# Two looked-up couples instead of three, warmed TensorE and fewer DMA additions in a field-pair recommendation tower

## The chip, the cores and the metric

The kernel is one launch on one core of a Trainium2 chip. The metric is the device time in microseconds. The core has five engines, each with its own in-order queue of instructions: TensorE (PE, matmuls; PEld is its weight load), VectorE (DVE), ScalarE (ACT), GpSimd (POOL) and SyncE (SP, which here only starts DMAs). They meet through semaphores. SBUF and PSUM are the two on-chip memories; TensorE writes only to PSUM, and GpSimd here reads and writes only SBUF.

## The reference

512 samples have 40 fields; each field has a table of 64-wide rows and one id per sample. For each of the 780 pairs of fields the row of the one goes through a 64 x 64 matrix of its own and is multiplied with the row of the other. The 780 values and 16 dense inputs go through three dense layers.

```python
e = jnp.stack([tbl_0[ids[:, 0]], tbl_1[ids[:, 1]], ...], axis=1)   # 512 x 40 x 64
vi, vj = e[:, i_idx, :], e[:, j_idx, :]                            # the 780 pairs
z = einsum('bpe,bpe->bp', einsum('bpd,pde->bpe', vi, W), vj)
h = concatenate([z, dense_ctx], axis=1)
h = maximum(h @ W_top1 + b_top1, 0.0)
h = maximum(h @ W_top2 + b_top2, 0.0)
y = h @ W_top3
```

## The kernel before

**Couples of fields.** The 40 fields are handled as 20 couples, each 128 numbers (two fields of 64) for 512 samples. They are taken from the last couple (fields 38 and 39) to the first. "Couple u" is the u-th to arrive, `k = KP - 1 - u` its place in the model. `E` is a ring of six slots that holds a couple as 128 x 512, fields down the partitions and samples across.

**Two ways to fetch a couple.** Couples 0 to 2 (`LOOKED_UP = 3`) come from small tables (1000 or 1250 rows), which are loaded whole. VectorE compares the ids with row numbers and so writes "codes", 125 x 512 matrices of zeros and ones (`encode`, L485); TensorE multiplies each part of the table with its code (`look_up_fields`, L550). There are 20, 18 and 16 such look-ups. The ids of the first couple are spread over the partitions by two matmuls (L641) and copied to SBUF by ScalarE (L421); those of the others are loaded by DMA, once per couple, ahead of its tables (L315, L319). The other couples are gathered: GpSimd starts eight indirect DMAs for each (two fields, four batches of 128 samples; `gather`, L369), and TensorE turns the rows with four transposes (`transpose_fields`, L561). ScalarE copies each couple out of PSUM into `E` (L400) and DMAs place pieces of it in `E4`.

**The main loop.** `order()` yields 37 couples of "groups" (74 groups, numbered n; a group is a set of field pairs), 13 "batched" units and the points at which couples of fields arrive. For a group TensorE makes two steps of products (`products`, L599) in a PSUM ring of three, VectorE multiplies each with other fields (`multiply`, L507), and seven groups later TensorE sums the result with ones (`reduce_two`, L624). For some couples of groups the two halves of the product are added before, so that the sum takes 8 instructions and not 16: by GpSimd (`ADDED_COUPLES`, L380) or by an accumulating DMA that GpSimd starts (`DMA_COUPLES`, L377). In a batched unit TensorE makes four steps (L582), VectorE multiplies (L521), and ScalarE sums eight fields of each with 16 short instructions per half (L416). The batched units multiply with the wide rows, samples down the partitions, of couples 0 to 3; looked-up couples are turned for this by TensorE (`turn_rows`, L570) and copied (L407).

**What sets the order.** Every engine follows `order()`. GpSimd runs through the groups in turn and puts ahead of group n all gathers with `gather_due(u, i) <= n`, which is `GATHER_LEAD` groups before they are wanted. Its DMA and its own additions stand in the same queue. `ahead(u)` says how many groups before its first use a couple of fields is turned. `SPLIT_FIRST` is the order in which ScalarE copies couples 0 to 3; the first group needs couples 2 and 3, the second also 1 and 0.

## Time and profile before

| | before |
|---|---|
| median of 3 runs | 329.62 us (329.34 to 329.81) |
| profiled execution: time, span | 329.33 us, 327.5 us |
| TensorE busy | 315.8 us, 96% |
| VectorE busy | 258.3 us, 79% |
| GpSimd busy | 234.9 us, 72% |
| ScalarE busy | 219.4 us, 67% |

A busy share is a mean over stages. TensorE's matmuls overlap and their ends are modelled, so 96% isn't a full engine. GpSimd's figure leaves out the 0.3 us between two gathers. What bounds a stage is read from what ended the idle time of an engine there, in brackets at the end of a timeline's row.

### The profile page before, as it was taken

The page shows a single profiled execution, that of the slowest core. Times are in us where ns is not written, and L with a number is a line of the kernel's source. Part 1 is how long each engine was busy: PE and PEld are TensorE (multiplying, and loading weights), DVE is VectorE, ACT ScalarE, POOL GpSimd, SP SyncE. Part 2 cuts the span into 40 slices and gives each one's busy share as a digit, 9 for nine tenths or more (in the row PEclk, how much of TensorE's full clock was granted, in tenths as well). Part 3 has the DMA queues.
Part 4 walks back from the last instruction along what each step waited for, and adds up shares of the span by engine and source line. Part 5 has one row for each costly group of instructions (what it writes and reads, how often), then busy time and mean ns, then how long its engine had stood idle before and what let it go on. Part 6 is the DMA issues. An engine that isn't in the chain of part 4 may idle for free.

```text
span 327.5 us, 5637 instructions
## 1 busy us (share of the span) xinstructions
PE 315.8 (96%) x1488; PEld 111.6 (34%) x1488; DVE 258.3 (79%) x270; ACT 219.4 (67%) x1699; POOL 234.9 (72%) x196
## 2 busy tenths in 40 slices
PE   6999999999999999999999999999999999999996
PEld 1232343333323324333224333332233333234442
DVE  3798379778888898998999899989999987960000
ACT  3000220049984999699999999999999999810022
POOL 6787777777788767779879998999999773940000
PEclk9999999999999999999999999999999999999999
DMA  3555825242579799994333223223212200000000
GB/s 96 142 151 147 236 73 148 68 133 70 127 163 186 185 209 256 285 258 115 79 83 88 84 56 108 79 77 79 73 42 82 64 1 0 3 2 0 0 0 0
DMA packets 19320, 33.16 MB, mean 101 GB/s; under 512 B 4948, under 2 KB 5080, under 8 KB 19288
## 3 DMA queue, kind: packets, MB, share of 16 engines
q1 hardware_dynamic: 12344, 21.52, 22.1%
q0 software_dynamic: 5792, 9.71, 15.5%
q10 hardware_dynamic: 1152, 1.57, 1.7%
q8 instruction: 12, 0.20, 0.3%
q14 instruction: 20, 0.16, 0.2%
HBM read 22.82 MB, written 0.00 MB: 70 GB/s over the span
## 4 chain that ended last, share of the span: by engine, by line
PE 73%; ACT 10%; DMA 8%; DVE 5%; issue 3%; SPq 1%; DVEq 0%
PE ps_t L599 33%; PE ps_z L624 12%; PE ps_t L582 12%; ACT batched L416 9%; DMA prod<-in_tbl 8%; PE ps_t L633 6%; DVE prod L507 4%; PE ps_e L561 3%; PE ps_t L550 2%; PE ps_t L688 2%; PE ps_e L633 2%; DVE batched L521 1%; ACT E L400 1%; PE ps_e L570 1%; PE ps_t L666 0%
## 5 line engine op out<-in xcount | busy, mean ns | idle before, releaser
L416 ACT ACTIVATE batched<-batched 128x64 f32<-128x64 f32 x832 | 198.8, 253 | 0.0
L507 DVE TENSOR_TENSOR prod<-ps_t,E 128x1024 f32<-128x1024 f32 x148 | 171.0, 1217 | 16.6 <-PE ps_t L599 16.0
L416 ACT ACTIVATION_READ_ACCUMULATOR batched<-batched 128x1 f32 x832 | 165.9, 199 | 0.0
L369 POOL DMA_INDIRECT rows<-in_tbl,ids_sb x128 | 125.5, 981 | 35.1 <-issue 34.7
L599 PE MATMUL ps_t<-E,w_sb 64*128 64x512 f32 x592 | 145.3, 614 | 4.2 <-ACT E L400 2.0
L380 POOL TENSOR_TENSOR prod<-prod 128x1024 f32<-128x1024 f32 x38 | 89.9, 2373 | 13.2 <-DVE prod L507 12.7
L599 PEld LDWEIGHTS ps_t<-E,w_sb 64*128 64x128 f32 x592 | 51.1, 185 | 86.9 <-issue 57.0
L521 DVE TENSOR_TENSOR batched<-ps_t,wide_rows 128x1024 f32<-128x1024 f32 x52 | 60.1, 1218 | 7.9 <-PE ps_t L582 7.6
L582 PE MATMUL ps_t<-w_sb,E 64*128 64x512 f32 x208 | 48.4, 603 | 0.0
L624 PE MATMUL ps_z<-prod,quads 128*32 128x512 f32 x320 | 48.1, 602 | 0.0
L400 ACT ACTIVATE E<-ps_e 128x512 f32<-128x512 f32 x18 | 10.6, 591 | 49.2 <-PE ps_e L561 36.0
L485 DVE TENSOR_SCALAR prod<-prod,first_row_f 125x512 f32<-125x512 int32 (+1 forms) x54 | 24.0, 504 | 8.4 <-ACT prod L421 4.0
L582 PEld LDWEIGHTS ps_t<-w_sb,E 64*128 64x128 f32 x208 | 18.5, 186 | 30.1 <-issue 21.0
L633 PE MATMUL ps_t<-z,w_sb 128*128 128x512 f32 (+1 forms) x42 | 18.4, 592 | 0.0
L624 PEld LDWEIGHTS ps_z<-prod,quads 128*32 128x32 f32 x320 | 8.7, 108 | 28.1 <-issue 15.0
L550 PE MATMUL ps_t<-prod 125*64 125x512 f32 x68 | 16.9, 596 | 0.4 <-DMA prod<-in_tbl 0.4
L624 PE MATMUL ps_z<-prod,halves 128*32 128x512 f32 x80 | 17.2, 598 | 0.0
L550 PE MATMUL ps_e<-prod 125*64 125x512 f32 x40 | 13.2, 751 | 0.6 <-DMA prod<-in_tbl 0.6
L377 POOL DMA_DIRECT2D prod<-prod x10 | 10.2, 1023 | 2.4 <-DVE prod L507 2.4
L633 PEld LDWEIGHTS ps_t<-z,w_sb 128*128 128x128 f32 (+1 forms) x42 | 8.0, 190 | 10.1 <-issue 10.1
L561 PE MATMUL ps_e<-ident,rows 128*128 128x128 f32 x64 | 10.5, 286 | 0.8 <-ACT wide_rows L407 0.8
L561 PEld LDWEIGHTS ps_e<-ident,rows 128*128 128x128 f32 x64 | 6.7, 140 | 12.8 <-issue 12.8
(43 smaller groups left out, 69.2 us busy)
## 6 DMA issues: line engine op xcount, KB each, us to landing
w_sb<-in_w_units SPq DMA_DIRECT2D x50, 256.0 KB, 2.7
prod<-prod POOLq DMA_DIRECT2D x10, 512.0 KB, 5.8
E<-E SPq DMA_DIRECT2D x48, 64.0 KB, 2.4
rows<-in_tbl,ids_sb POOLq DMA_INDIRECT x128, 3.3
w_sb<-in_w SPq DMA_DIRECT2D x7, 256.0 KB
E<-E ACTq DMA_DIRECT2D x24, 64.0 KB, 3.7
prod<-in_ids_by_field SPq DMA_DIRECT2D x2, 512.0 KB, 4.4
prod<-in_tbl SPq DMA_DIRECT2D x3, 312.5 KB
```

Of the source, the lines that this page charges most:

```text
L369: pool.indirect_dma_start(rows_of(u, b)[:, f * DIM:(f + 1) * DIM], None, tables[2 * k + f], bass.IndirectOffsetOnAxis(ap=ids_sb[:, col:col ...
L380: pool.tensor_tensor(prod[:, n % P_RING, 0, :, :], prod[:, n % P_RING, 0, :, :], prod[:, n % P_RING, 1, :, :], ALU.add).then_inc(halves_ad ...
L416: last = act.activation(products, products, ACT.Copy, accum_out=zt[:, b, at:at + 1])
L485: dve.tensor_scalar(codes[0:used, j % CODE_RING, :], wide, float(c), first_row_f[0:used, i:i + 1], ALU.subtract, ALU.is_equal).then_inc(co ...
L507: dve.tensor_tensor(prod[:, n % P_RING, s, :, :], ps_t[:, step % STEPS, :, :], multiplier, ALU.mult).then_inc(product_ready, 1)
L521: dve.tensor_tensor(batched[:, at % B_RING, :, :, :].rearrange("p i f n -> p i (f n)"), ps_t[:, step % STEPS, :, :], wide_rows[:, b, None, ...
L550: pe.matmul(e_bank[u][half:half + DIM, :], small[f][:, c, :], codes[0:splits[f][0], j % CODE_RING, :], start=(c == 0), stop=(c == splits[f ...
L561: last = pe.transpose(e_bank[u][:, b * P:(b + 1) * P], rows_of(u, b), ident[:])
L582: last = pe.matmul(ps_t[:, step % STEPS, i, :], E[at:at + DIM, slot_of(k), b * P:(b + 1) * P], w_sb[at:at + DIM, m % W_RING, :], start=Tru ...
L599: last = pe.matmul(ps_t[:, step % STEPS, j, :], w_sb[at:at + DIM, m % W_RING, col:col + P], E[at:at + DIM, slot_of(pairs_of(n)[s][j]), :], ...
L624: last = pe.matmul(ps_z[to:to + 32, :], ones, prod[:, g % P_RING, s, j, :], start=(q == 0 and s == 0), stop=((q == PER_CHUNK // 2 - 1 or n ...
L633: last = pe.matmul(h1_bank[m], w1_sb[0:used, c, m * P:(m + 1) * P], z[0:used, c, :], start=(c == 0), stop=(c == ALL_CHUNKS - 1))
```

## The change

- Two couples are looked up instead of three (38 look-ups instead of 54). Couple 2 is gathered as couple 3 is, with eight more gathers (144 instead of 136). Couple 2 is turned before the first look-up of couple 1 and couple 3 before its seventeenth.
- Three matmuls of the identity with itself stand ahead of TensorE's first work.
- The codes of couple 0 are made straight from PSUM; ScalarE's two copies are gone.
- ScalarE's queue starts the load of one of the first two tables. SyncE starts the weights when three of the four tables and the ids have landed.
- Couples 7 and 8 of groups (groups 14 to 17) are not halved any more; `DMA_COUPLES` is 10, 11, 13.
- Couple 6 of the fields is turned one group earlier; couples are copied in the order 0, 2, 3, 1; wide rows are turned twice instead of three times, one group later; gathers are due 8 groups ahead instead of 7.

```diff
-FETCHED_AT = 8
-LOOKED_UP = 3
+FETCHED_AT = (0, 16)
+LOOKED_UP = 2
+WARM_UP = 3
-GATHER_LEAD = 7
+GATHER_LEAD = 8
-DMA_COUPLES = (7, 8, 10, 11, 13)
+DMA_COUPLES = (10, 11, 13)
 def ahead(u):
-    return 0 if u in (6, 7) else 1 if u < 12 else 2
+    return 0 if u == 7 else 1 if u < 12 else 2
-SPLIT_FIRST = (0, 1, 3, 2)
+SPLIT_FIRST = (0, 2, 3, 1)
-WIDE_AFTER = (0, 1, 2)
+WIDE_AFTER = (1, 2)
...
 # SyncE
-            for u in range(LOOKED_UP):
-                if u > 0:
-                    for f in looked_up[2 * u - 2:2 * u]:
-                        sp.wait_ge(small_loaded[f], 16)
-                    sp.dma_start(ids_wide[:, 2 * u:2 * u + 2, :].bitcast(I32),
...
+            load_small(looked_up[0])
+            for f in looked_up[0:2]:
+                sp.wait_ge(small_loaded[f], 16)
+            for u in range(1, LOOKED_UP):
+                sp.dma_start(ids_wide[:, 2 * u:2 * u + 2, :], ids_by_field[None, looked_up[2 * u]:looked_up[2 * u] + 2, :].
+                             to_broadcast([P, 2, BATCH])).then_inc(wide_loaded[u], 16)
                 for f in looked_up[2 * u:2 * u + 2]:
+                    load_small(f)
+                sp.wait_ge(wide_loaded[u], 16)
...
-            for f in looked_up:
+            for f in looked_up[:-1]:
                 sp.wait_ge(small_loaded[f], 16)
...
 # ScalarE
+            f = looked_up[1]
+            act.dma_start(small[f], tables[f].rearrange("(p c) n -> p c n", p=splits[f][0])).then_inc(small_loaded[f], 16)
...
-            for i in range(2):
-                act.wait_ge(ids_spread, i + 1)
-                act.activation(ids_wide[:, i, :], ps_t[:, 0, i, :], ACT.Copy).then_inc(ids_spread_copied, 1)
...
 # VectorE
-                        dve.wait_ge(ids_spread_copied, i + 1)
-                    wide = ids_wide[0:used, i, :] if u == 0 else ids_wide[0:used, i, :].bitcast(I32)
+                        dve.wait_ge(ids_spread, i + 1)
+                    wide = ps_t[0:used, 0, i, :] if u == 0 else ids_wide[0:used, i, :]
...
 # TensorE
-                    if u == LOOKED_UP - 1 and j - before == FETCHED_AT:
-                        transpose_fields(LOOKED_UP)
+                    if u == 1 and j - before in FETCHED_AT:
+                        transpose_fields(LOOKED_UP + FETCHED_AT.index(j - before))
...
+            for _ in range(WARM_UP):
+                pe.matmul(ps_z[:, 0:P], ident[:], ident[:], start=True, stop=True)
```

**TensorE, from its first look-up to its first products.** Before (L550 is a look-up, L561 a transpose of gathered rows, L599 a product; `small_loaded34` is the table of field 34):

```order
L550 MATMUL ps_e<-prod 64x512 [waits code_ready,small_loaded38,sums_ready]
L550 MATMUL ps_e<-prod 64x512 [waits code_ready,small_loaded39]
L550 MATMUL ps_e<-prod 64x512 [waits code_ready] x18
L550 MATMUL ps_t<-prod 64x512 [waits code_ready,small_loaded36]
L550 MATMUL ps_t<-prod 64x512 [waits code_ready,small_loaded37]
L550 MATMUL ps_t<-prod 64x512 [waits code_ready] x16
L550 MATMUL ps_t<-prod 64x512 [waits code_ready,small_loaded34]
L550 MATMUL ps_t<-prod 64x512 [waits code_ready,small_loaded35]
L550 MATMUL ps_t<-prod 64x512 [waits code_ready] x6
L561 MATMUL ps_e<-ident,wide_rows 128x128 [waits e_copied,wide_rows_loaded3]
L561 MATMUL ps_e<-ident,wide_rows 128x128 x3
L550 MATMUL ps_t<-prod 64x512 [waits code_ready] x8
```

The same place now (L553, L564 and L602 are the three lines above):

```order
L553 MATMUL ps_e<-prod 64x512 [waits code_ready,small_loaded38,sums_ready]
L553 MATMUL ps_e<-prod 64x512 [waits code_ready,small_loaded39]
L553 MATMUL ps_e<-prod 64x512 [waits code_ready] x18
L564 MATMUL ps_t<-ident,wide_rows 128x128 [waits wide_rows_loaded2]
L564 MATMUL ps_t<-ident,wide_rows 128x128 x3
L553 MATMUL ps_t<-prod 64x512 [waits code_ready,small_loaded36]
L553 MATMUL ps_t<-prod 64x512 [waits code_ready,small_loaded37]
L553 MATMUL ps_t<-prod 64x512 [waits code_ready] x14
L564 MATMUL ps_e<-ident,wide_rows 128x128 [waits e_copied,wide_rows_loaded3]
L564 MATMUL ps_e<-ident,wide_rows 128x128 x3
L553 MATMUL ps_t<-prod 64x512 [waits code_ready] x2
L602 MATMUL ps_t<-E,w_sb 128x512 [waits e_copied,w_loaded0]
```

The look-ups of fields 34 and 35 are gone, and four transposes of couple 2's gathered rows stand before those of field 36.

**GpSimd, from its first gather on.** Before (each L369 row is a run of gathers, L377 an accumulating DMA; `transposed` is TensorE's count of couples turned):

```order
L369 DMA wide_rows<-in_tbl,ids_sb 128x64 [waits ids_loaded]
L369 DMA wide_rows<-in_tbl,ids_sb 128x64 x7
L369 DMA rows<-in_tbl,ids_sb 128x64 x32
L369 DMA rows<-in_tbl,ids_sb 128x64 [waits transposed]
L369 DMA rows<-in_tbl,ids_sb 128x64 x7
L369 DMA rows<-in_tbl,ids_sb 128x64 [waits transposed]
L369 DMA rows<-in_tbl,ids_sb 128x64 x7
L369 DMA rows<-in_tbl,ids_sb 128x64 [waits transposed]
L369 DMA rows<-in_tbl,ids_sb 128x64 x7
L369 DMA rows<-in_tbl,ids_sb 128x64 [waits transposed]
L369 DMA rows<-in_tbl,ids_sb 128x64 x4
L377 DMA prod<-prod 128x1024 [waits product_ready]
```

Now (L372 gathers, L380 is the DMA), the first and then the last rows ahead of the first DMA:

```order
L372 DMA wide_rows<-in_tbl,ids_sb 128x64 [waits ids_loaded]
L372 DMA wide_rows<-in_tbl,ids_sb 128x64 x15
L372 DMA rows<-in_tbl,ids_sb 128x64 x32
L372 DMA rows<-in_tbl,ids_sb 128x64 [waits transposed]
```

```order
L372 DMA rows<-in_tbl,ids_sb 128x64 [waits transposed]
L372 DMA rows<-in_tbl,ids_sb 128x64 x7
L372 DMA rows<-in_tbl,ids_sb 128x64 [waits transposed]
L372 DMA rows<-in_tbl,ids_sb 128x64 x3
L380 DMA prod<-prod 128x1024 [waits product_ready]
```

The eight gathers of couple 2 stand ahead of all others, and 92 gathers stand ahead of the first DMA (for group 20), where 69 stood ahead of the first one before (for group 14).

**TensorE at couple 6 of the fields.** Before (L624 is a sum of products; `rows_loaded2` are couple 6's rows):

```order
L624 MATMUL ps_z<-prod,halves 32x512 [waits product_ready]
L624 MATMUL ps_z<-prod,halves 32x512 x7
L599 MATMUL ps_t<-E,w_sb 128x512 [waits product_ready,e_copied,w_loaded4]
L599 MATMUL ps_t<-E,w_sb 128x512
L599 MATMUL ps_t<-E,w_sb 128x512 [waits product_ready]
L599 MATMUL ps_t<-E,w_sb 128x512
L561 MATMUL ps_e<-ident,rows 128x128 [waits e_copied,rows_loaded2]
L561 MATMUL ps_e<-ident,rows 128x128 x3
```

Now:

```order
L627 MATMUL ps_z<-prod,halves 32x512 [waits product_ready]
L627 MATMUL ps_z<-prod,halves 32x512 x7
L564 MATMUL ps_e<-ident,rows 128x128 [waits e_copied,rows_loaded2]
L564 MATMUL ps_e<-ident,rows 128x128 x3
L602 MATMUL ps_t<-E,w_sb 128x512 [waits product_ready,e_copied,w_loaded4]
L602 MATMUL ps_t<-E,w_sb 128x512
L602 MATMUL ps_t<-E,w_sb 128x512 [waits product_ready]
L602 MATMUL ps_t<-E,w_sb 128x512
```

The transposes moved ahead of group 8.

## Rows read from the trace of the kernel before

**Rows 1.** Timeline of TensorE: start, us, instructions [idle before <-releaser].

```profile
33.40 3.65 PE L550 MATMUL ps_t<-prod 125*64 125x512 f32 x16
37.87 1.99 PE L599 MATMUL ps_t<-E,w_sb 64*128 64x512 f32 x8 [0.81 <-ACT E L400]
...
50.42 0.66 PE L561 MATMUL ps_e<-ident,rows 128*128 128x128 f32 x4
```

**Rows 2.** Chain that ended last, in order of time: start, us, what.

```profile
19.37 9.82 DMA prod<-in_tbl
```

**Rows 3.** Granted clock in 40 slices; weight loads of the look-ups.

```profile
PEclk9999999999999999999999999999999999999999
...
13.36 0.24 PEld L550 LDWEIGHTS ps_e<-prod 125*64 125x64 f32 x2 [0.62 <-DVE prod L485]
14.09 0.14 PEld L550 LDWEIGHTS ps_e<-prod 125*64 125x64 f32 x2 [0.49 <-issue]
```

**Rows 4.** Timeline of GpSimd.

```profile
3.33 1.10 POOL L369 DMA_INDIRECT wide_rows<-in_tbl,ids_sb  x1 [1.28 <-DMA ids_sb<-in_ids_t]
...
19.10 1.18 POOL L369 DMA_INDIRECT rows<-in_tbl,ids_sb  x1 [0.30 <-issue]
...
35.42 0.94 POOL L369 DMA_INDIRECT rows<-in_tbl,ids_sb  x1 [0.30 <-issue]
...
92.56 1.02 POOL L377 DMA_DIRECT2D prod<-prod  x1
```

**Rows 5.** Timeline of TensorE at the transposes of couples 6 to 9.

```profile
58.94 1.99 PE L599 MATMUL ps_t<-E,w_sb 64*128 64x512 f32 x8
60.86 0.66 PE L561 MATMUL ps_e<-ident,rows 128*128 128x128 f32 x4
...
69.61 0.66 PE L561 MATMUL ps_e<-ident,rows 128*128 128x128 f32 x4
...
78.40 0.66 PE L561 MATMUL ps_e<-ident,rows 128*128 128x128 f32 x4
...
88.54 0.66 PE L561 MATMUL ps_e<-ident,rows 128*128 128x128 f32 x4
```

**Rows 6.** Row gathers issued in 24:35, 60:92 and 65.3:66.3: count, median us to landing.

```profile
rows<-in_tbl,ids_sb POOLq DMA_INDIRECT x8, 6.0
...
rows<-in_tbl,ids_sb POOLq DMA_INDIRECT x27, 2.6
...
rows<-in_tbl,ids_sb POOLq DMA_INDIRECT x1, 2.7
```

**Rows 7.** The chain at couple 13: start, us, what.

```profile
137.91 0.60 ACT E L400
138.50 21.02 ACT batched L416 x176
```

**Rows 8.** Groups by form: xcount | busy, mean ns | idle before.

```profile
L507 DVE TENSOR_TENSOR prod<-ps_t,E 128x1024 f32<-128x1024 f32 x148 | 171.0, 1217 | 16.6 <-PE ps_t L599 16.0 <-issue 0.4
...
L485 DVE TENSOR_SCALAR prod<-prod,first_row_f 125x512 f32<-125x512 int32 x34 | 15.1, 508 | 2.1 <-PE ps_t L550 2.1
...
L485 DVE TENSOR_SCALAR prod<-prod,first_row_f 125x512 f32<-125x512 f32 x20 | 8.8, 497 | 6.2 <-ACT prod L421 4.0 <-PE ps_e L550 2.3
```

**Rows 9.** Timeline of TensorE: a sum of 16, one of 8, later products.

```profile
96.53 1.92 PE L624 MATMUL ps_z<-prod,quads 128*32 128x512 f32 x16
...
112.77 1.06 PE L624 MATMUL ps_z<-prod,quads 128*32 128x512 f32 x8
...
123.46 3.70 PE L599 MATMUL ps_t<-E,w_sb 64*128 64x512 f32 x16
```

**Rows 10.** Timeline of VectorE at group couples 7 and 8.

```profile
115.01 4.62 DVE L521 TENSOR_TENSOR batched<-ps_t,wide_rows 128x1024 f32<-128x1024 f32 x4
...
124.70 4.62 DVE L507 TENSOR_TENSOR prod<-ps_t,E 128x1024 f32<-128x1024 f32 x4 [0.55 <-PE ps_t L599]
```

**Rows 11.** Accumulating DMAs issued in 122:123 and 125.7:126: KB, us to landing.

```profile
prod<-prod POOLq DMA_DIRECT2D x1, 512.0 KB, 8.6
...
prod<-prod POOLq DMA_DIRECT2D x1, 512.0 KB, 10.1
```

**Rows 12.** GpSimd's own additions, group of the page: busy, mean ns, idle before.

```profile
L380 POOL TENSOR_TENSOR prod<-prod 128x1024 f32<-128x1024 f32 x38 | 89.9, 2373 | 13.2 <-DVE prod L507 12.7
```

More of the change, by code:

```diff
@@ L204, in tower_kernel @@
             at += c * DIM
-        ids_wide = scratch[:, at:at + len(looked_up) * BATCH].rearrange("p (f n) -> p f n", f=len(looked_up))
+        ids_wide = scratch[:, at:at + len(looked_up) * BATCH].bitcast(I32).rearrange(
+            "p (f n) -> p f n", f=len(looked_up))
         at += len(looked_up) * BATCH
@@ L241, in tower_kernel @@
         ids_spread = sem("ids_spread")
-        ids_spread_copied = sem("ids_spread_copied")
         small_loaded = {f: sem(f"small_loaded{f}") for f in looked_up}
```

6 lines of the change are left out of this document (2 added, 4 removed).

## The prediction

> **What bounds the kernel now.** The timeline of TensorE comes first [rows 1]: look-ups (L550) until 37.1 us, products (L599) from 37.87. The look-ups wait for tables: the third load alone is 9.82 us in the chain of waits [rows 2]. They also start at half rate: weight loads last 0.24 us at 13.4 and 0.14 from 14.09, though the granted clock reads 9 tenths or more, the upper level of 2.4 GHz, in every slice [rows 3].
>
> Next GpSimd [rows 4]. It gathers without a pause: 45 gathers start from 35.42 on, the last just before 92.56, so one every 1.249 us, and each couple of fields needs eight, 10 us. TensorE turns a couple (L561) when its rows are there: couple 6 at 60.9, 7 at 69.61, 8 at 78.40, 9 at 88.54 [rows 5]. In the kernel before, couple 8's last gather starts at 35.42 + 24 x 1.249 = 65.4 and lands 2.7 us later (a look at that one; median 2.6 from 60 to 92 us, 6.0 from 24 to 35 [rows 6]), at 68.1: 10 us early. No engine's wait ends with these rows. That lead is what the change spends.
>
> Until 137 us TensorE paces VectorE; ScalarE waits for couple 13's transposes until 137.91 and then goes straight into 21 us of sums [rows 7]. All later work hangs on couple 13, and the tail stays as it is. So the question is when couple 13 is turned.
>
> **The front.** 16 of 54 look-ups go, at 3.65 us for 8 [rows 1] 7 us, and the third table load with its 9.82. Couples 2 and 3 are now gathered before and beside the look-ups; couple 3's last gather is the sixteenth: 3.33 + 15 x 1.249 + about 1 of slowness (below) = 23.1, landing up to 6.0 later [rows 4, 6], 29.1. Transposes 0.6, two look-ups 0.9 and a copy 0.6 put the first products at about 31, 7 us earlier. Tables don't forbid it: the second load is issued by 9.1 as before, takes 9.82 at most, and 18 look-ups of 0.45 end at 27. The warm-up, the codes read from PSUM, the second queue for a table and the two dropped copies of ids (0.60 each) all lie ahead of that wait, so I cost them at nothing. Without that cover the codes are the doubtful one. Nearest rows: 0.50 us for a code from SBUF, 1.217 for 1024 elements from PSUM, half of which is 0.61 [rows 8]. I take 0.61 (same memory): 2.2 us more over 20 codes, bounds 0 and 14 (0.50 to 1.217 each). The Trainium skill, VectorE: DVE Perf Modes, Why PSUM operands drop a tier, says that a float32 operand in PSUM gets no doubled rate; that speaks against this edit, and agrees with 0.61 rather than 0.50. The wait for couple 3's rows covers it.
>
> **What is late next: the gathers.** Two couples are gathered ahead of couple 4 instead of one, so every later couple sits eight gathers further back. Couple 5's last gather gets the slot that starts at 45.4 now, 6's that of 55.4, 7's 65.4, 8's 75.4, 9's 85.4. The slots themselves move a little. From 3.33 to 35.42 are 23 intervals; at 1.249 they would take 28.7, they took 32.1: 3.4 us of slowness. Of it 2.6 fall between 19.10 and 35.42 (16.3 us for 11 intervals), where a gather lasts 1.18 instead of 0.94 while VectorE writes codes from int32 ids [rows 4, 8]. 34 such codes become 18, so 2.6 becomes 1.4. With 0.2 for the start (1.10 instead of 0.94), 3.4 becomes 1.6, and the slots are 1.75 us earlier. Bounds: 0 (the slowness stays whole) and 3.2 (all but the start goes).
>
> The rule that bears on this is in the Trainium skill, SBUF — State Buffer, section SBUF: two separate sides: a VectorE instruction that uses both ports locks GpSimd out, and it can't write DMA descriptors meanwhile. The trace agrees in that gathers last longer beside codes and 0.94 elsewhere. By the rule codes from PSUM don't lock, which leaves the same 1.6 within 0.2.
>
> So couple 8's rows land at 75.4 - 1.75 + 2.75 = 76.4. Now TensorE. Couple 5 lands at 46.4, and TensorE has turned couple 4 and done its two groups at about 43: it stands still some 4 us. From 46.4 it takes 8.5 us to couple 6 (50.42 to 58.94, since couple 6 now comes one group earlier), 54.9; its rows land at 56.4. From 56.4 transposes 0.6, two groups 3.8, sums 1.85 and a batched unit 3.6 make 66.3; couple 7's rows land at 66.4. From there 8.8 us (69.61 to 78.40 [rows 5]) to 75.2, and again it waits, for couple 8, until 76.4. From there 10.1 us (78.40 to 88.54) to couple 9, 86.5; its rows land at 86.4. The lead is then 88.5 - 86.5 = 2.0 us. All but 2 of the front's 7 us are gone, and whether products start at 28 or 34 doesn't matter. Couples 10 to 12 have their rows in time (couple 11: slot 105.3 - 1.75 + 3.3 = 106.9, wanted at 108.3).
>
> **Group couples 7 and 8, no longer halved.** The sum of each takes 16 instructions instead of 8: 1.92 against 1.06 in the timeline, +0.86 [rows 9]. The first stands ahead of the batched unit whose first product VectorE takes at 115.01 without a gap, just as TensorE has it ready: it moves by 0.86. The second stands ahead of the products of 123.46, for which VectorE idles 0.55 [rows 10]: in full again. Cost 1.7 us, bounds 0.9 (one hidden) and 1.8. The four accumulating DMAs that go take GpSimd 1.02 us each [rows 4], off the path. GpSimd now has 92 gathers before its first DMA: 3.33 + 1.6 + 91 x 1.249 + 0.95 = 119.5. That of group 21 starts two gathers and a DMA later, 123.2; from 122.2 to 123 one took 8.6 us to land [rows 11], so 131.8, and TensorE wants it at 132.6. Hidden, nothing added. Later, GpSimd carries 10.0 us of gathers more, 4.1 of DMAs and 1.75 of slowness less: 4.1 against the 13.2 that it idles ahead of its own additions [rows 12]. Hidden too.
>
> **Sum.** 1.7 - 2.0 = -0.3 us at couple 13 and at the end. The profiled execution took 329.33 us (span 327.5 and 1.8 around it), so 329.0; the median of the runs is 0.3 higher: 329.3.
>
> **Rivals.**
> 1. *The gathers win back more.* The slowness goes but for the start (3.2), rows land after 2.35: couple 8 at 74.5, a lead of 3.9, less 1.7: 2.2 faster, 327.4. For it: 0.94 us whenever VectorE writes no codes. Against: 18 int32 codes stay.
> 2. *The gathers win back nothing* (the slower side). The slots stay: couple 8 lands at 78.1, lead 0.3, time +1.4, 331.0. Slower from slots less than 0.8 us earlier on. For it: weights are now loaded beside the gathers of couples 3 and 4, and beside such loads a landing took 6.0. Against: couple 8 is gathered long after.
> 3. *TensorE cools in its new wait.* Before, no gap after 14 us is over 0.81; now one is about 4. If it costs what the start shows (5 us at half rate, so 2.5), couple 6 is turned at 57.9 instead of 56.4, couple 8 at 76.9: lead 1.5, 329.8. The Trainium skill, TensorE: Matmul & The Clock Gate, What's actually happening, has the clock fall to half after idling; no row of before has such a gap.
> 4. *The DMA additions come late.* A landing of 10.1, as from 125.7 [rows 11], puts group 21's at 133.3: +0.7, 330.0 and more with rival 3.
> 5. *The front's gain passes through*: 7 - 1.7, 324.3. It needs gathers faster than one in 1.249 us, which no row has. Here "the front gets shorter" and "the time falls" part.
>
> **Chances.** A measurement can tell about 0.2%, 0.66 us, from no change. Forecast (lead 1.1 to 2.4): 0.44, all within 0.2%; rival 1: 0.22; rival 5: 0.03; rival 2: 0.15; rivals 3 and 4, alone or with a smaller lead: 0.16, of which 0.04 stay within 0.2%. Faster 0.25, same 0.48, slower 0.27. The range goes from rival 1 to rival 2 with most of rival 4 on top: 327.3 to 331.5. The forecast's own is 328.7 to 330.2.
>
> **What would show it.** First products near 31 us; TensorE idle some 4 us before couple 5's transposes near 46, and again, by 1 to 1.5, before those of couples 6 and 8 at 56.4 and 76.4, each time until row gathers land; GpSimd's 56th gather at 73.6; transposes of couple 9 at 86.5, of couple 13 at 136.9. Weight loads of 0.24 us after 46 would be rival 3. The forecast is wrong if couple 8 is turned before 75.5 or after 77.5, or if TensorE loses other than 1.7 us between couples 9 and 13.

## The result: 1.1% slower, where no change was forecast

| | before | after |
|---|---|---|
| median of the runs | 329.66 us (329.34 to 329.81) | 333.72 us (331.83 to 333.89, 4 runs) |
| profiled execution: time, span | 329.33, 327.5 us | 333.67, 331.8 us |
| 1st, 24th, 56th, 64th gather starts | 3.33, 35.42, 75.38, 85.38 | 6.24, 38.23, 78.15, 88.15 |
| couple 9 turned, couple 13 turned | 88.54, 137.21 | 91.51, 141.90 |

The kernel before ran beside the kernel after once more, hence 329.66. The ratio of the times is 1.0114 [1.0092, 1.0137], so the change costs 4 us. The forecast was 329.3, with a range of 327.3 to 331.5. One execution of E3 below took 390.74 us at a granted clock of 0.76; it is left out of E3's median and ratio, and all other runs are in.

The page of the kernel after: its span, the granted clock in 40 slices, and the chain that ended last by engine.

```profile
span 331.8 us, 5589 instructions
...
PEclk9999896999999999999999999999999999999999
...
PE 55%; POOL 19%; ACT 9%; issue 8%; DVE 5%; DMA 2%; SPq 0%; DVEq 0%
```

The front no longer ends in TensorE's own work: 19% of the chain is now GpSimd. Where it passes shows in its longest pieces (start, us, what).

```profile
1.17 4.80 DMA ids_sb<-in_ids_t
20.14 3.29 POOL wide_rows L372
88.15 3.32 DMA rows<-in_tbl,ids_sb
```

From the load of the gathers' ids the chain goes through every gather up to the 64th, which starts at 88.15, then through the landing of its rows into the transposes of couple 9. The timeline of GpSimd at these places, which answers to [rows 4]:

```profile
6.24 1.10 POOL L372 DMA_INDIRECT wide_rows<-in_tbl,ids_sb  x1 [4.46 <-DMA ids_sb<-in_ids_t]
...
20.14 3.29 POOL L372 DMA_INDIRECT wide_rows<-in_tbl,ids_sb  x1 [0.30 <-issue]
...
38.23 0.94 POOL L372 DMA_INDIRECT rows<-in_tbl,ids_sb  x1 [0.30 <-issue]
...
78.15 0.94 POOL L372 DMA_INDIRECT rows<-in_tbl,ids_sb  x1 [0.30 <-issue]
...
88.15 0.95 POOL L372 DMA_INDIRECT rows<-in_tbl,ids_sb  x1 [0.30 <-issue]
```

Between the 24th and the 64th gather 40 slots take 49.92 us, 1.248 each, as before (1.249). What differs is where they begin: 2.9 us later, since the ids landed 4.80 us after their issue instead of 1.9. And the first 24 gathers lose 3.3 us, as much as before (3.4), though there are 18 int32 codes and not 34: one gather alone lasts 3.29 us. TensorE, which answers to [rows 1, 5]:

```profile
30.78 0.66 PE L564 MATMUL ps_e<-ident,wide_rows 128*128 128x128 f32 x4 [2.20 <-DMA wide_rows<-in_tbl,ids_sb]
...
34.08 4.50 PE L602 MATMUL ps_t<-E,w_sb 64*128 64x512 f32 x16
...
50.63 1.12 PE L564 MATMUL ps_e<-ident,rows 128*128 128x128 f32 x4 [3.92 <-DMA rows<-in_tbl,ids_sb]
51.68 7.64 PE L602 MATMUL ps_t<-E,w_sb 64*128 64x512 f32 x24
...
61.11 0.66 PE L564 MATMUL ps_e<-ident,rows 128*128 128x128 f32 x4
...
70.82 0.66 PE L564 MATMUL ps_e<-ident,rows 128*128 128x128 f32 x4
...
80.59 0.66 PE L564 MATMUL ps_e<-ident,rows 128*128 128x128 f32 x4 [0.91 <-DMA rows<-in_tbl,ids_sb]
...
91.51 0.66 PE L564 MATMUL ps_e<-ident,rows 128*128 128x128 f32 x4 [0.71 <-DMA rows<-in_tbl,ids_sb]
...
141.90 0.66 PE L564 MATMUL ps_e<-ident,rows 128*128 128x128 f32 x4
```

The brackets are what the prediction asked for: products begin 3.8 us earlier than before (34.08 against 37.87), and then TensorE stands still until rows land, at 50.63, 80.59 and 91.51. At couple 9 it is 2.97 us behind before; at couple 13 it is 4.69 behind, so 1.72 came between. From couple 13 to the end of the span are 189.9 us, against 190.3 before.

The clock, by stretch (us; busy us and count of PE, PEld, DVE, ACT, POOL; granted clock; share and GB/s of DMA):

```profile
32.00:36.00 4.00, 4.00 (x10) 1.19 (x9) 0.00 (x0) 0.67 (x2) 3.09 (x4) 0.57 0.40 90
...
47.00:50.00 3.00, 0.00 (x0) 0.00 (x0) 1.80 (x2) 0.00 (x0) 2.39 (x3) 0.90 0.45 120
50.00:56.00 6.00, 5.37 (x14) 2.59 (x16) 1.71 (x2) 0.60 (x1) 4.48 (x6) 0.50 0.26 67
```

After the two long waits the granted clock is 0.57 and 0.50, the lower of the two levels (1.2 GHz); 24 products at 51.68 take 7.64 us. Behind the shorter waits (0.7 to 0.9) it stays at the upper one. The page's PEclk line shows it only as an 8 and a 6.

### The profile page after: what moved, and what is told of

Same layout as the page of the kernel before. It is cut to its first block, busy times and chain, and to the rows that moved or that the text cites. A ratio compares the mean times of both kernels' runs of the same rounds, so it can differ in the third digit from the quotient of the medians.

```text
span 331.8 us, 5589 instructions
## 1 busy us (share of the span) xinstructions
PE 314.7 (95%) x1478; PEld 113.9 (34%) x1478; DVE 255.4 (77%) x254; ACT 217.6 (66%) x1696; POOL 237.5 (72%) x198
## 3 DMA queue, kind: packets, MB, share of 16 engines
q1 hardware_dynamic: 11810, 20.16, 19.9%
## 4 chain that ended last, share of the span: by engine, by line
PE 55%; POOL 19%; ACT 9%; issue 8%; DVE 5%; DMA 2%; SPq 0%; DVEq 0%
PE ps_t L602 24%; POOL rows L372 13%; PE ps_z L627 10%; PE ps_t L585 9%; ACT batched L422 9%; POOL wide_rows L372 6%; PE ps_t L636 5%; DVE prod L510 4%; PE ps_t L693 2%; PE ps_e L636 2%; PE ps_e L564 2%; DMA ids_sb<-in_ids_t 1%; DMA rows<-in_tbl,ids_sb 1%; DVE batched L524 1%; ACT E L406 0%
## 5 line engine op out<-in xcount | busy, mean ns | idle before, releaser
L422 ACT ACTIVATION_READ_ACCUMULATOR batched<-batched 128x1 f32 x832 | 157.0, 189 | 0.0
L602 PE MATMUL ps_t<-E,w_sb 64*128 64x512 f32 x592 | 147.1, 624 | 2.6 <-issue 0.7
L372 POOL DMA_INDIRECT rows<-in_tbl,ids_sb x128 | 122.1, 954 | 35.2 <-issue 35.0
L602 PEld LDWEIGHTS ps_t<-E,w_sb 64*128 64x128 f32 x592 | 52.4, 190 | 87.2 <-issue 58.9
L627 PE MATMUL ps_z<-prod,quads 128*32 128x512 f32 x336 | 49.9, 601 | 0.0
L372 POOL DMA_INDIRECT wide_rows<-in_tbl,ids_sb x16 | 18.4, 1148 | 9.0 <-issue 4.6
L564 PE MATMUL ps_e<-ident,rows 128*128 128x128 f32 x64 | 10.9, 295 | 6.3 <-DMA rows<-in_tbl,ids_sb 5.5
L488 DVE TENSOR_SCALAR prod<-ps_t,first_row_f 125x512 f32<-125x512 f32 x20 | 13.3, 740 | 3.1 <-PE ps_t L646 3.1
L553 PE MATMUL ps_e<-prod 125*64 125x512 f32 x40 | 12.6, 694 | 1.2 <-DMA prod<-in_tbl 1.2
L564 PEld LDWEIGHTS ps_e<-ident,rows 128*128 128x128 f32 x64 | 7.0, 145 | 18.6 <-DMA rows<-in_tbl,ids_sb 9.6
L452 ACT ACTIVATE E<-ps_e,b_sb 128x512 f32<-128x512 f32 x1 | 0.7, 687 | 15.2 <-PE ps_e L636 15.2
```

The source lines that it names most:

```text
L372: pool.indirect_dma_start(rows_of(u, b)[:, f * DIM:(f + 1) * DIM], None, tables[2 * k + f], bass.IndirectOffsetOnAxis(ap=ids_sb[:, col:col ...
L422: last = act.activation(products, products, ACT.Copy, accum_out=zt[:, b, at:at + 1])
L488: dve.tensor_scalar(codes[0:used, j % CODE_RING, :], wide, float(c), first_row_f[0:used, i:i + 1], ALU.subtract, ALU.is_equal).then_inc(co ...
L553: pe.matmul(e_bank[u][half:half + DIM, :], small[f][:, c, :], codes[0:splits[f][0], j % CODE_RING, :], start=(c == 0), stop=(c == splits[f ...
L564: last = pe.transpose(e_bank[u][:, b * P:(b + 1) * P], rows_of(u, b), ident[:])
L602: last = pe.matmul(ps_t[:, step % STEPS, j, :], w_sb[at:at + DIM, m % W_RING, col:col + P], E[at:at + DIM, slot_of(pairs_of(n)[s][j]), :], ...
```

## The experiments

Fourteen kernels ran. "Slowness" is the time from the first to the 24th gather less 23 intervals of 1.249 us. All places are from the one profiled execution of each kernel; E1's took 329.58 us, 1.1 below its median, and E9's 336.84, 2.6 above. The ratio is against the kernel before, run on the same chip (medians there 329.35 to 329.66).

| | edit | median us, ratio [95%] | 1st, 24th gather | slowness | couple 9, 13 |
|---|---|---|---|---|---|
| before | | 329.66 | 3.33, 35.42 | 3.4 | 88.54, 137.21 |
| after | | 333.72, 1.0114 [1.0092, 1.0137] | 6.24, 38.23 | 3.3 | 91.51, 141.90 |
| E1 | after, table back on SyncE | 330.65, 1.0019 [1.0, 1.0037] | 3.31, 33.62 | 1.6 | 87.03, 137.42 |
| E2 | after, weights later | 332.71, 1.0086 [1.0054, 1.0119] | 6.57, 37.38 | 2.1 | 90.77, 141.16 |
| E4 | after, codes from SBUF | 332.06, 1.0076 [1.005, 1.0101] | 6.08, 36.21 | 1.4 | 89.50, 140.13 |
| E6 | E1 and E4 | 330.22, 1.0018 [1.0006, 1.003] | 3.29, 34.73 | 2.7 | 87.74, 138.70 |
| E10 | after, no warm-up | 332.25, 1.0099 [1.0061, 1.0138] | 6.11, 36.25 | 1.4 | 89.50, 139.88 |
| E11 | E1, float32 ids | 332.14, 1.0084 [1.0056, 1.0113] | 3.25, 36.67 | 4.7 | 89.89, 140.28 |
| E13 | E1, all codes from PSUM | 327.75, 0.9947 [0.993, 0.9963] | 3.31, 32.19 | 0.15 | 85.85, 136.24 |
| E3 | after, couples 7, 8 by DMA | 337.22, 1.0203 [1.0176, 1.023] | | | |
| E9 | E1, couples 7, 8 by DMA | 334.27, 1.0128 [1.0106, 1.015] | 3.30, 35.40 | 3.4 | 88.80, 145.08 |
| E7 | before, couples 7, 8 whole | 331.81, 1.0082 [1.0064, 1.01] | 3.26, 35.50 | 3.5 | 89.29, 139.68 |
| E8 | before, table on ScalarE | 328.57, 0.9973 [0.9956, 0.999] | 5.96, 36.72 | 2.0 | 87.34, 136.01 |
| E5 | before's three, new front | 327.13, 0.9934 [0.9919, 0.9948] | 3.29, 35.38 | 3.4 | 86.26, 134.93 |
| E12 | E5, 12 more identities | 328.43, 0.9965 [0.9949, 0.9981] | 3.26, 34.87 | 2.9 | 87.38, 136.05 |
| E14 | E5, 6 more identities | 329.31, 0.9995 [0.9978, 1.0011] | 3.29, 36.55 | 4.5 | 88.01, 136.68 |

**E1: the ids come first again.** SyncE starts both first tables, behind `ids_sb`; ScalarE starts none.

```diff
             load_small(looked_up[0])
+            load_small(looked_up[1])
...
-            f = looked_up[1]
-            act.dma_start(small[f], tables[f]...).then_inc(small_loaded[f], 16)
```

> Only ScalarE's early load of field 39's table goes back to SyncE's queue, behind the ids. Late-ids theory: in the changed kernel the first gather starts at 6.24 instead of 3.33, because this table's transfer is already under way when the ids are requested; with it behind them the first gather starts at 3.3, every slot up to couple 9 is 2.9 us earlier, couple 9 is turned near 88.6 instead of 91.5, and the time falls by 2.9 us, 333.7 to about 330.8. Rival, cold clock: the loss is from TensorE's half rate in its new waits; then the ids don't matter and the time stays within 0.7 us of 333.7. Rival, slow gather: the one gather of 3.29 us at 20.14 stays wherever it falls, so the gain is 2.9 and not 5.

Timeline of GpSimd in E1:

```profile
3.31 1.10 POOL L373 DMA_INDIRECT wide_rows<-in_tbl,ids_sb  x1 [1.52 <-DMA ids_sb<-in_ids_t]
...
21.10 2.07 POOL L373 DMA_INDIRECT wide_rows<-in_tbl,ids_sb  x1 [0.30 <-issue]
...
33.62 0.94 POOL L373 DMA_INDIRECT rows<-in_tbl,ids_sb  x1 [0.30 <-issue]
```

The first gather is back at 3.31. The 24th is 4.6 us earlier than in after and couple 9 is turned 4.5 earlier (87.03 against 91.51): 2.9 us from the ids, as expected, and 1.7 because the slowness is 1.6 us in this execution instead of 3.3 (its long gather lasts 2.07). Over all ten runs the median falls by 3.1 us. One line of code, which starts 312 KB from another queue at 0.74 us, ahead of an 80 KB load, is the larger part of the loss of 4 us.

**E8: the same line put into the kernel before.**

```diff
-                for f in looked_up[2 * u:2 * u + 2]:
+                for f in looked_up[2 * u:2 * u + (1 if u == 0 else 2)]:
...
+            f = looked_up[1]
+            act.dma_start(small[f], tables[f]...).then_inc(small_loaded[f], 16)
```

> The kernel before with one edit: field 39's table is started by ScalarE's queue, as in the kernel after. Theory (the second queue delays ids_sb, and that costs time only where the gathers have no lead): ids_sb lands some 2.9 us later, the first gather starts near 6.2 instead of 3.3, the slots from the 24th gather on sit 2 to 3 us later, but couple 8's rows, now 10 us early, are still 7 early, so no wait of TensorE ends with row gathers and couple 9 is turned at 88 to 89 as before: 329.3 to 330.3. Of these up to 0.7 would come from the DMA additions of groups 14 to 17, whose place in GpSimd's queue is 2 to 3 us later. Rival (the table by ScalarE is itself dear, whatever the lead): time follows the slots, 332 or more.

Timelines of GpSimd and then TensorE in E8:

```profile
5.96 1.10 POOL L369 DMA_INDIRECT wide_rows<-in_tbl,ids_sb  x1 [3.91 <-DMA ids_sb<-in_ids_t]
```

```profile
36.66 1.99 PE L602 MATMUL ps_t<-E,w_sb 64*128 64x512 f32 x8 [0.81 <-ACT E L403]
...
87.34 0.65 PE L564 MATMUL ps_e<-ident,rows 128*128 128x128 f32 x4
```

The ids are 2.6 us late here too, and no wait of TensorE ends with rows. The time doesn't stay where I expected it (329.3 to 330.3). It falls, because the tables come sooner on two queues and the third no longer makes TensorE wait; products start 1.2 us earlier and couple 9 is turned 1.2 earlier. So the same line gains 0.8 us in the median where the gathers have 10 us of lead and costs three where they have none.

**E2: weights later.** SyncE waits for all 38 codes before it starts the weights, to see whether their traffic holds up the long gather.

```diff
             for f in looked_up[:-1]:
                 sp.wait_ge(small_loaded[f], 16)
+            sp.wait_ge(code_ready, 38)
```

> SyncE starts the six first weight loads only when all 38 codes are made (about 27 us instead of 15.65). Traffic theory: the gather that lasted 3.29 us at 20.14 was slowed by the weight loads (DMA share 1.0 from 17 to 21 us); without them it lasts 1.0, slots are 2.0 to 2.3 us earlier, time 331.5 or so. Port theory: VectorE writes int32 codes one behind the other from 19.77 and keeps GpSimd off the shared port; then one gather stays at about 3.3 and the time is 333.7, or more if products now wait for weights (27 + 5 = 32 against first products at 34.08: no wait expected).

A gather of 2.73 us at 20.46 stays, before any weight is loaded (27.95). Timeline of GpSimd in E2, and the stretch of that gather as in the table of the clock above:

```profile
20.46 2.73 POOL L373 DMA_INDIRECT wide_rows<-in_tbl,ids_sb  x1 [0.30 <-issue]
```

```profile
20.40:23.20 2.80, 2.80 (x13) 1.05 (x14) 2.80 (x8) 0.60 (x1) 2.73 (x1) 1.00 0.05 12
```

The DMA engines are 5% busy meanwhile, so neither weights nor any other load is its cause. VectorE is busy all the time. The 332.71 us lie between the two times expected, and the interval overlaps that of after.

**E4: couple 0's codes from SBUF again.** ScalarE copies the spread ids and VectorE reads the copies.

```diff
-                        dve.wait_ge(ids_spread, i + 1)
-                    wide = ps_t[0:used, 0, i, :] if u == 0 else ids_wide[0:used, i, :]
+                        dve.wait_ge(ids_spread_copied, i + 1)
+                    wide = ids_wide[0:used, i, :].bitcast(F32) if u == 0 else ids_wide[0:used, i, :]
```

> ScalarE copies the first couple's ids to SBUF again and VectorE reads them there. Codes of couple 0 go back from 0.66 us apart to 0.43. Gather-bound theory: couple 0's look-ups end some 3 us earlier, the int32 codes start some 3 us earlier, first products don't move by more than 1 us since they wait for couple 3's rows, and the time stays within 0.7 of 333.7. Rival, codes from PSUM cost time: 1 us or more faster. Port theory of the 3.3 us gather: it moves with the start of the int32 codes, to about 17 us.

No gather lasts over 1.25 us, the slots are 2.0 us earlier than in after, and the time fell by 1.7 where at most 0.7 was expected. It looked as if reading PSUM made the long gather; E13 below, with all codes from PSUM and no long gather, shows that this alone doesn't. A part of the gain is lost again at a DMA addition, in the chain and the timeline of TensorE in E4:

```profile
125.67 9.70 DMA prod<-prod
```

```profile
135.50 1.06 PE L631 MATMUL ps_z<-prod,quads 128*32 128x512 f32 x8 [0.18 <-DMA prod<-prod]
```

**E6: E1 and E4 together.**

> The changed kernel with both repairs: field 39's table by SyncE behind the ids, and the ids copied to SBUF. Each alone gave 3.1 and 1.7 us. Theory: late ids (2.9 us of slots) and one gather held for 2 to 3 us while int32 codes are written back to back are separate and both move the slots of couples 8 and 9, so the two add up: first gather at 3.3, no gather over 1.3, couple 9 turned near 86.5, and 333.7 - 3.1 - 1.7 = 328.9, or 328.3 since the DMA addition for group 21 that TensorE waited for in the second is 2.9 us earlier too. Rival: both work through the same wait and the second adds nothing: 330.6.

The two repairs don't add: 330.22, hardly below E1, and the rival said 330.6. With the ids early again most of the first 24 gathers stand beside codes that are read from SBUF, the slowness is 2.7 us, and a DMA addition ends 0.50 of TensorE's wait at 134.07. No gather lasts over 1.28 us; the slowness is made of many that last 1.18 to 1.28. The expectation was 1.3 to 1.9 us too low.

**E10: no warm-up.** `WARM_UP = 0`.

> The kernel after without the three matmuls of the identity. Theory (the warm-up lies off the path, since the gathers set when couples 5 and 9 are turned): first products within 1.5 us of 34.1, couple 9 turned at 91.5 within 0.3, time 333.7 within 0.7. Rival (the warm-up pays for itself in the first look-ups and that reaches the end): 334.7 or more.

First products come at 31.13 and couple 9 is turned at 89.50, not near 34.1 and at 91.5. In this execution no gather lasts over 1.28 us, though VectorE writes the same codes. The intervals of E10 and of after overlap, and after itself has runs at 331.83 and at 333.67 to 333.89, about as far apart as one long gather. So the long gather is probably there in some executions only (argued from the times, since one execution of each kernel was profiled), and no effect of the warm-up can be seen.

**E11: float32 ids.** E1, and VectorE turns couple 1's ids into float32 once; the 18 codes read that copy.

```diff
                     dve.wait_ge(wide_loaded[u], 16)
+                    dve.tensor_copy(ids_wide[:, 0:2, :].bitcast(F32), ids_wide[:, 2:4, :]).then_inc(wide_cast, 1)
+                    dve.wait_ge(wide_cast, 1)
```

> The variant of the kernel after in which SyncE again starts both first tables (codes of couple 0 still from PSUM), with one more edit: VectorE first turns couple 1's ids from int32 into float32, once, and its 18 codes read float32 from SBUF. Theory (the slow gather belongs to int32 codes written back to back): no gather between the first and the 24th lasts over 1.3 us (2.07 at 21.10 without the edit), the slowness from the first to the 24th falls from 1.59 us to about 0.6, the slots are 0.5 to 1.0 us earlier and the time is 0.3 to 1.0 us less than 330.65. Rival (it belongs to reading PSUM before, or to what the DMA queues carry, not to the type): a gather of 2 us or more stays, and the time is 330.65 within 0.3.

The theory that int32 is at fault falls: 332.14 us, 1.5 more than E1 where 0.3 to 1.0 less was expected. Timelines of GpSimd and of VectorE in E11:

```profile
22.79 4.84 POOL L374 DMA_INDIRECT wide_rows<-in_tbl,ids_sb  x1 [0.30 <-issue]
```

```profile
20.16 7.35 DVE L489 TENSOR_SCALAR prod<-prod,first_row_f 125x512 f32<-125x512 f32 x18
```

It is the longest gather of all, and the two rows suggest what it waits for: VectorE writes 18 codes from SBUF without a pause from 20.16 to 27.51, and the gather that starts at 22.79 ends at 27.63, 0.12 us behind the last code.

**E13: no code from SBUF at all.** E1, and TensorE spreads the ids of both couples; all 38 codes are read from PSUM.

```diff
-            sp.dma_start(ids_first[:], ids_by_field[looked_up[0]:looked_up[0] + 2, :])...
+            sp.dma_start(ids_first[:], ids_by_field[36:40, :])...
...
-            for i in range(2):
-                pe.matmul(ps_t[:, 0, i, :], pick[:, i, :], ids_first_f[:], ...)
+            for i in range(4):
+                pe.matmul(ps_t[:, i // 2, i % 2, :], pick[:, looked_up[i] - 36, :], ids_first_f[:], ...)
...
-                    wide = ps_t[0:used, 0, i, :] if u == 0 else ids_wide[0:used, i, :]
+                    wide = ps_t[0:used, u, i % 2, :]
```

> The variant of the kernel after in which SyncE again starts both first tables, with one more edit: the ids of couple 1 are spread over the partitions by TensorE as well (two more matmuls of 0.95 us), so that all 38 codes are read from PSUM and none from SBUF; the 512 KB load of couple 1's ids goes. Theory (a gather is held up while VectorE reads codes from SBUF without a pause, whatever their type, and by how much differs from one execution to the next): every gather between the first and the 24th lasts 0.94 to 0.96 us but the first, slowness 0.2 to 0.4 us instead of 1.4 to 4.9; codes 0.66 us apart end near 32; couple 9 turned at 85.5 to 86.2, couple 13 1.72 + 48.67 later, near 136.2, time 328.5 to 329.5, and the runs lie within 0.8 us of each other instead of 2 to 2.6. Rival (the long gather comes from the DMA queues or from the code before it): one gather of 2 us or more stays in some executions, time 330 or more or a spread over 1.5 us.

Timelines of GpSimd, VectorE and TensorE in E13:

```profile
3.31 1.10 POOL L370 DMA_INDIRECT wide_rows<-in_tbl,ids_sb  x1 [1.53 <-DMA ids_sb<-in_ids_t]
...
22.21 0.94 POOL L370 DMA_INDIRECT wide_rows<-in_tbl,ids_sb  x1 [0.30 <-issue]
...
32.19 0.94 POOL L370 DMA_INDIRECT rows<-in_tbl,ids_sb  x1 [0.30 <-issue]
```

```profile
15.65 17.87 DVE L481 TENSOR_SCALAR prod<-ps_t,first_row_f 125x512 f32<-125x512 f32 x27 [0.30 <-PE ps_e L546]
```

```profile
35.70 1.99 PE L595 MATMUL ps_t<-E,w_sb 64*128 64x512 f32 x8
38.64 1.99 PE L595 MATMUL ps_t<-E,w_sb 64*128 64x512 f32 x8 [0.95 <-ACT E L401]
...
85.85 0.66 PE L557 MATMUL ps_e<-ident,rows 128*128 128x128 f32 x4
...
136.24 0.66 PE L557 MATMUL ps_e<-ident,rows 128*128 128x128 f32 x4
```

Every gather but the first lasts 0.94 or 0.95 us, though VectorE writes 27 codes without a pause beside them; the slowness is 0.15 us. The runs lie 1.1 us apart, a little more than the 0.8 I wrote. Codes of 0.66 us put the first products at 35.70, 1.6 us later than in after, and the second ones at 38.64, behind a copy by ScalarE. Yet no wait of TensorE ends with rows any more, and it is the fastest kernel with two looked-up couples: 327.75 us, which by the distances from the kernel before is 5.7 less than after. Couple 9 and couple 13 come 5.7 us earlier too. It keeps the whole 1.72 us of group couples 7 and 8 (85.85 to 136.24 are 50.39). The 512 KB load of couple 1's ids is gone as well, and the two weren't tried apart; E2's long gather, beside idle DMA engines, speaks against the load.

The Trainium skill, SBUF — State Buffer, section SBUF: two separate sides, has VectorE and GpSimd share a port pair, held for the whole of an instruction. The runs agree with such a lock, but here it is not one instruction of 0.5 us that keeps a gather out: in E11 it is a run of them, for 4.84 us.

**What starts a long gather isn't settled.** Seven kernels read couple 0's codes from PSUM and couple 1's from SBUF (after, E1, E2, E3, E9, E10, E11). In all but E10 a gather of 2.07 to 4.84 us starts within 2.7 us of the switch. Eight read every code from SBUF; there E14 has one of 2.87 and E12 one of 1.67, and the other six none over 1.28. So the switch is a rival, or a part of the cause, that no run tests. E3 shows the same places as E11, in the execution with the low clock (timelines of VectorE and GpSimd):

```profile
19.75 2.85 DVE L488 TENSOR_SCALAR prod<-prod,first_row_f 125x512 f32<-125x512 int32 x7
```

```profile
20.06 2.66 POOL L372 DMA_INDIRECT wide_rows<-in_tbl,ids_sb  x1 [0.30 <-issue]
```

The seven codes last 0.48 us each and start 0.40 apart, each before the last has ended, and the gather ends 0.12 us behind the seventh. E5 has runs of seven as close as this (from 17.27 to 20.12, say) and no long gather, so that isn't enough either.

**E7: the unhalved couples alone.** Before, with `DMA_COUPLES = (10, 11, 13)`.

> The kernel before with only this part of the change: couples 7 and 8 of groups not halved. Theory: two sums of 1.92 instead of 1.06 us on TensorE, both on its path, nothing else: +1.7 us, 331.35. Rival: GpSimd's queue, four DMAs shorter, gives some of it back, or one of the two sums is hidden: at most +0.9.

Timeline of TensorE in E7:

```profile
89.29 0.66 PE L561 MATMUL ps_e<-ident,rows 128*128 128x128 f32 x4
...
139.68 0.66 PE L561 MATMUL ps_e<-ident,rows 128*128 128x128 f32 x4
```

From couple 9 to couple 13 are 50.39 us against 48.67 before, 1.72 more. The other 0.75 us lie ahead of couple 9: in this execution its third tables landed 0.7 us later. The edit touches nothing there. But all six runs are at least 2.2 us above the median of before on that chip (the median 2.46, where 1.7 was expected), so chance in one execution doesn't explain it, and why the front was slower stays open.

**E3 and E9: the other way round, couples 7 and 8 halved by DMA again.** `DMA_COUPLES = (7, 8, 10, 11, 13)` in after (E3) and in E1 (E9).

> Couples 7 and 8 of groups are halved by DMA again, the rest is the changed kernel. Theory: each sum goes from 1.92 back to 1.06 us and all of it is on the path between couples 9 and 13 (50.46 us in the changed kernel, 48.7 in the one before), so 1.7 us less: 332.0. Rival: GpSimd is later than before in this stretch, its four extra DMAs push the gathers of couples 12 and 13 or the additions of groups 20 to 23 past their due time, and at least half of the 1.7 is lost: 332.9 or more.

> Field 39's table by SyncE behind the ids (that alone took 330.65) and couples 7 and 8 of groups halved by DMA. With the late ids the same halving cost 3.8 us instead of giving 1.7. Queue theory: gathers of eight groups of lead stand ahead of the DMAs in GpSimd's queue, which comes to them at 105 to 119 us and has the sums of couples 7 and 8 (near 113 and 123) wait for the landing; with all slots 2.9 us earlier the wait shrinks by about that, so it costs 0 to 1 instead of 3.8: 330.7 to 331.7. Rival, the DMAs themselves slow TensorE or VectorE by traffic: +3.8 again, 334.4.

E3 is 3.5 us slower than after where I expected 1.7 faster. Its profiled execution is the one of 390.74 us, so E9 has to show why. Timeline of TensorE in E9:

```profile
116.15 1.06 PE L625 MATMUL ps_z<-prod,quads 128*32 128x512 f32 x8 [3.05 <-DMA prod<-prod]
...
139.06 1.93 PE L625 MATMUL ps_z<-prod,quads 128*32 128x512 f32 x8 [3.03 <-DMA prod<-prod]
```

With eight more gathers ahead, GpSimd issues the first of these additions at 106.27; in E5, with three looked-up couples, it is at 96.26, and no wait ends with one. The first wait ends with an addition for group couple 7. The second ends with the last one for couple 10, issued at 129.48: the added DMAs pushed it back in the queue. Two waits of 3 us are the price; couples 9 to 13 take 56.28 us instead of E1's 50.39. The queue theory had the place right and the size wrong (330.7 to 331.7 expected, 334.27 measured). The rival's 334.4 was met, but not for its reason: the waits end with landings, not with slower work. So the 1.72 us were not a mistake of the change: with GpSimd's queue as long as this the alternative costs more.

**E5: three looked-up couples, and of the change what isn't tied to two.** As E6 (codes from SBUF, the warm-up, loads in E1's order, the weights one table earlier, couple 6 one group earlier, a gather lead of 8), but with before's three couples, order of copies and DMA additions.

```diff
-FETCHED_AT = (0, 16)
-LOOKED_UP = 2
+FETCHED_AT = (8,)
+LOOKED_UP = 3
-DMA_COUPLES = (10, 11, 13)
+DMA_COUPLES = (7, 8, 10, 11, 13)
```

> Three couples are looked up and couples 7 and 8 of groups halved by DMA, as before; of the change it keeps the warm-up matmuls, the loads that no longer wait for the tables ahead of them (third ids and tables issued when the second ids have landed, near 13.6, instead of 18.6), the earlier couple 6 and the 8 groups of lead. Both tables of couple 0 are loaded by SyncE behind the ids, and the ids are copied to SBUF. Lead theory: the kernel before has 10 us of lead in its gathers and the change had to pay for its shorter front by spending it; a shorter front at 136 gathers keeps most of it. Look-ups: couple 0 ends near 18.5, then 34 look-ups of 0.43 and four transposes make 33.7, first products near 34.5 instead of 37.87; couple 8's rows (68) and 9's (78) are there long before, so 3.4 us pass through, and 0.7 more for the earlier couple 6: 329.6 to about 325.7. Rival, all gains of a front are lost in the main loop whatever the lead: 329.6.

Timeline of TensorE in E5:

```profile
36.54 1.99 PE L604 MATMUL ps_t<-E,w_sb 64*128 64x512 f32 x8 [0.81 <-ACT E L405]
...
86.26 0.66 PE L566 MATMUL ps_e<-ident,rows 128*128 128x128 f32 x4
...
134.93 0.66 PE L566 MATMUL ps_e<-ident,rows 128*128 128x128 f32 x4
```

327.13 us, the fastest here and faster than both kernels. Its slots are those of before (24th gather at 35.38, slowness 3.4), and that doesn't matter with 8 us of lead: products start 1.3 us earlier, couple 9 comes 2.3 earlier, and from there to couple 13 are before's 48.67. The expectation (products at 34.5, time 325.7) was 2.0 and 1.4 us too low. What the warm-up, the order of loads and the earlier couple 6 give each wasn't tried apart. The spreads of the runs don't follow the lead: 0.45 us here and 2.1 in after, but 2.1 in E14, whose lead is 9 us, and 0.3 in E11, which has none.

**E12 and E14: warm until the tables land.** Twelve and six more identity matmuls in E5, and the tables of fields 36 and 37 ahead of their ids.

```diff
+            for _ in range(12):
+                pe.matmul(ps_z[:, 0:P], ident[:], ident[:], start=True, stop=True)
             pe.wait_ge(sums_ready, 6)
```

> The variant with three looked-up couples and the new front (327.13 us), with two more edits: twelve more matmuls of the identity after the ids are spread, so that TensorE is busy until the first table lands at 9.2 us, and SyncE starts the tables of fields 36 and 37 ahead of their 512 KB of ids. Theory (the first five look-ups at half rate cost about 0.43 us each, and the chain then waits for a table until 19.32): weight loads of the first look-ups last 0.14 instead of 0.24 us, the table of field 36 lands before 18 us, first products at 34.5 to 35.5 instead of 36.54, time 325.3 to 326.5. Rival (couple 1's ids land later than they are wanted, or the DMA additions of groups 14 to 17 keep their place in GpSimd's queue while TensorE comes earlier to them, and take the gain back): 327 or more, with a wait of TensorE that ends with such a DMA.

> The variant with three looked-up couples, identity matmuls until the tables land and the tables of fields 36 and 37 ahead of their ids, now with six more identity matmuls instead of twelve (which ran from 6.81 to 11.69 us at 0.41 each and held up the look-ups from 9.25 to 11.62). Theory: they end near 9.3 us, when the first table is there; look-ups run at full rate without a gap, first products at 35.2 to 35.8, couple 9 turned 1.2 us before the 86.26 of the variant with three looked-up couples and the new front, time 325.7 to 326.5. Rival (DMA additions of groups 14 to 17 or look-ups that wait for field 36's table take it back): 327 or more, with a wait of TensorE that ends with a DMA.

Timeline of TensorE in E12:

```profile
6.81 4.88 PE L654 MATMUL ps_z<-ident 128*128 128x128 f32 x24
11.62 8.80 PE L559 MATMUL ps_e<-prod 125*64 125x512 f32 x40
```

The look-ups do run at full rate (40 matmuls in 8.80 us, 0.14 for a weight load), but the twelve took 4.88 us and end 2.4 us after 9.25, where E5 goes on with its look-ups. E14 takes six and fails elsewhere. Its timelines of TensorE and VectorE:

```profile
29.66 3.65 PE L559 MATMUL ps_t<-prod 125*64 125x512 f32 x14 [1.31 <-DMA prod<-in_tbl]
```

```profile
18.47 9.69 DVE L494 TENSOR_SCALAR prod<-prod,first_row_f 125x512 f32<-125x512 int32 x24 [1.03 <-DMA prod<-in_ids_by_field]
```

The ids, now behind two tables, make VectorE wait 1.03 us, and the third pair, which SyncE starts only when they are there, makes TensorE wait 1.31: products at 38.30. The rival's kind of loss was right, its place wrong: it is the third pair's table, neither field 36's nor an addition. The exchange of tables and ids and the identities weren't tried apart, so what the warmth alone is worth stays open; E12 bounds it: 54 look-ups without a gap from 11.62 to 36.8.

## Why the prediction was wrong

**The step that failed** is "the slots are 1.75 us earlier". They are 2.77 later (78.15 against 75.38 for the 56th), 4.5 us from the forecast. It had two halves.

- *The ids.* The prediction took the first gather to stay at 3.33 and cost "the second queue for a table" at nothing, since with the rest of the front it would "all lie ahead of that wait" of the look-ups. It does, for TensorE. But the same line also stands ahead of `ids_sb`, the load that the gathers wait for: the first gather starts at 6.24 instead of 3.33, 2.9 us (E1 takes them away, E8 puts 2.6 into before). The prediction itself had named the gathers as what is late next; it didn't ask what now stands ahead of the first DMA that they need.
- *The slowness.* "3.4 becomes 1.6" scaled before's loss by the number of int32 codes. It stayed 3.3 us in after, at the bound that the prediction gave (the slowness stays whole), and was 1.6 and 1.4 in E1 and E10. The number and the type of codes don't set it: E11, with no int32 code, has 4.7. Codes from PSUM cost the gathers nothing (E13: 0.15 us); while VectorE reads them from SBUF without a pause one gather may be shut out for 1 to 4 us beyond its 0.94. The size was off by 1.7 us in the profiled execution.

To this come 0.6 us from the last landing (3.32 and not 2.75). With the measured numbers the prediction's own sum comes out: a lead of 2.0 - 4.5 - 0.6 = -3.1 at couple 9 (measured -2.97), and 1.7 + 3.1 = 4.8 at couple 13 (measured 4.69). 0.35 us of it are won back later.

**Couple 9 hangs on the gathers**: right. In the eight kernels with two looked-up couples other than E13 and E3 it is turned 3.1 to 3.5 us after the 64th gather starts, whatever the front does (after 88.15 and 91.51, E1 83.56 and 87.03, E9 85.36 and 88.80).

**Group couples 7 and 8: +1.7**: right to 0.02 us, in after and in E7. **All later work hangs on couple 13**: right, 189.9 to 190.4 us in every kernel read here.

**The front**: products at 34.08 and not near 31, because the sixteenth gather came late. As foreseen it didn't matter. A code from PSUM costs 0.66 us from one to the next (740 ns each), near the 0.61 taken. But codes from SBUF follow each other after 0.43 (7.7 us for 18), not after the 0.50 that one lasts, so 20 codes cost 4.6 us more and not 2.2. The wait for couple 3's rows covered that too. The row of after by form, beside the codes from SBUF:

```profile
L488 DVE TENSOR_SCALAR prod<-ps_t,first_row_f 125x512 f32<-125x512 f32 x20 | 13.3, 740 | 3.1 <-PE ps_t L646 3.1
...
L488 DVE TENSOR_SCALAR prod<-prod,first_row_f 125x512 f32<-125x512 int32 x18 | 7.7, 499 | 0.0
```

**The rivals.** Rival 2 (the gathers win back nothing) ended on the right side, but its reason, weights beside gathers, is refuted by E2, and it stopped at slots that stay where they are; nothing in the range had them later than before. Rival 3 happened in part: the clock did fall to its lower level after waits of 2.2 and 3.9 us, but couples 6 and 7 are turned without a wait at 61.11 and 70.82 and couple 8 waits 0.91 again. From couple 5 to couple 6 are 10.5 us instead of the 8.5 taken; the 2.0 were absorbed by the next wait for rows. Rival 4 didn't decide in after, but did in E4 and E6 by 0.2 to 0.5 us, and in E9 by twice 3. Neither rival 5 nor rival 1 came. Rival 1's point, 0.94 us whenever VectorE writes no codes, holds in E13 even beside codes, when they are read from PSUM.

## What to carry to other kernels

When a change spends the lead of a queue, price everything that stands ahead of that queue's first instruction, down to the load of its indices, and take its irregularities in full: with 10 us in hand the line that made a load late gave a gain (E8), with none it cost 3 us. Keep the first small load of the longest chain ahead of large ones on every queue, not only on its own. A slower operand that leaves a shared port alone (codes of 0.66 us from PSUM for codes of 0.43 from SBUF) can be the faster choice, if the engine at the other end of the port is the one that sets the end.
